# The Gelu table's load behind the last use of ACT in a batch, and the router's rows turned in the banks of the second product

## The reference

```python
edge_index = jnp.stack([src, dst])          # 100000 edges, sorted by dst
x = x + gnn(layernorm(x), edge_index, ...)  # 8 heads
x = x + experts(layernorm(x)[None], ...)[0] # 8 experts, 2 a token
```

```python
out = agg + xn @ W_res + bias
out = layer_norm(out, ln2_g, ln2_b)
ff = gelu_tanh(out @ ffn_w1 + ffn_b1) @ ffn_w2 + ffn_b2   # 256 -> 1024 -> 256
return out + ff
```

## Time and profile before

| | |
|---|---|
| median of 3 executions | 3304.02 us (3302.67 to 3306.39) |
| profiled execution, its own time | 3309.24 us |
| its span | 3307.6 us |
| mean granted clock of TensorE over the span | 0.75 |
| busy: PE, DVE, ACT, POOL | 2076.5, 1683.3, 1450.4, 1175.7 us |
| edges and before | 2204 us |
| layer stage | 413 us |
| experts | 691 us |

### The profile page before, as it was taken

One profiled execution on the slowest core, in us unless ns is written; L12 is line 12 of the kernel. 1 busy time (PEld: TensorE's weight loads), 2 busy tenths in 40 slices (PEclk: granted clock), 3 DMA queues, 4 the chain that ended last, 5 costly groups with the idle time before them and its releaser, 6 DMA issues.

```text
span 3307.6 us, 51219 instructions
## 1 busy us (share of the span) xinstructions
PE 2076.5 (63%) x16490; PEld 1777.0 (54%) x16490; DVE 1683.3 (51%) x5236; ACT 1450.4 (44%) x3212; POOL 1175.7 (36%) x1155
## 2 busy tenths in 40 slices
PE   5334554445544455444554445469899499999999
PEld 4223333334333343333433333358878499999999
DVE  6234554445544455444554445587766445555554
ACT  3313333333333333333333333346665466666665
POOL 2444334433344333443344433301323312222223
PEclk8656666666666666666666666679999799999999
DMA  7633333333333333333333333322222444463533
GB/s 187 174 99 91 96 95 105 112 88 96 95 108 99 98 96 95 109 99 98 94 96 109 99 98 88 95 94 65 91 73 67 136 108 97 77 171 51 146 50 40
DMA packets 268719, 329.50 MB, mean 100 GB/s; under 512 B 118550, under 2 KB 207984, under 8 KB 263716
## 3 DMA queue, kind: packets, MB, share of 16 engines
q0 software_dynamic: 63840, 151.61, 19.3%
q1 hardware_dynamic: 204036, 173.54, 17.5%
q10 hardware_dynamic: 576, 1.09, 0.1%
HBM read 431.90 MB, written 95.53 MB: 159 GB/s over the span
## 4 chain that ended last, share of the span: by engine, by line
PE 41%; another core or an unknown queue 30%; DVE 10%; issue 8%; ACT 7%; DMA 1%; SPq 1%; DVEq 1%; POOL 1%; ACTq 0%; POOLq 0%
PE bank L928 14%; PE bank L1104 7%; PE bank L1105 7%; PE bank L1106 7%; PE bank L917 2%; ACT edge_mem L827 1%; DVE edge_mem L994 1%; ACT layer_hid L1199 1%; DVE seg_max L1031 1%; PE bank L514 1%; ACT layer_mem L1198 1%; DVE win_mem L1020 1%; ACT layer_mem L1207 1%; DVE piece_lo L1100 1%
## 5 line engine op out<-in xcount | busy, mean ns | idle before, releaser
L737 POOL DMA_INDIRECT edge_mem<-node_table,src_col x880 | 836.5, 951 | 1188.9 <-PE bank L928 923.0
L928 PE MATMUL bank<-edge_mem 128*128 128x264 f32 x1760 | 554.5, 488 | 4.6 <-DVE edge_mem L994 3.3
L1104 PE MATMUL bank<-expert_rounded 128*128 128x256 f32 x1792 | 509.0, 284 | 34.9 <-DVE expert_rounded L1100 30.2
L1105 PE MATMUL bank<-expert_rounded 128*128 128x256 f32 x1792 | 508.7, 284 | 0.0
L1106 PE MATMUL bank<-expert_rounded 128*128 128x256 f32 x1792 | 508.5, 284 | 0.0
L1041 DVE TENSOR_TENSOR exponent<-edge_mem,bank 128x128 f32<-128x128 f32 x55 | 15.8, 288 | 928.7 <-remote 926.6
L928 PEld LDWEIGHTS bank<-edge_mem 128*128 128x128 f32 x1760 | 429.6, 249 | 108.2 <-issue 5.0
L917 PE MATMUL bank<-cand,edge_mem 128*128 128x9 bf16 x2640 | 81.2, 169 | 644.0 <-DVE cand L1054 618.0
L843 ACT CAST cand<-bank 128x128 bf16<-128x128 f32 x55 | 14.8, 268 | 1019.2 <-remote 1005.2
L917 PEld LDWEIGHTS bank<-cand,edge_mem 128*128 128x128 bf16 x2640 | 75.4, 104 | 682.6 <-DVE cand L1054 655.6
L1104 PEld LDWEIGHTS bank<-expert_rounded 128*128 128x128 f32 x1792 | 345.7, 193 | 35.1 <-issue 35.1
(11 more groups left out here) (229 smaller groups left out, 3968.0 us busy)
## 6 DMA issues: line engine op xcount, KB each, us to landing
expert_rounded<-split_w SPq DMA_DIRECT2D x224, 1024.0 KB
split_w<-piece_hi SPq DMA_DIRECT2D x72, 256.0 KB
split_w<-piece_lo SPq DMA_DIRECT2D x72, 256.0 KB
piece_full<-in_L_ffn_W SPq DMA_DIRECT2D x64, 256.0 KB
expert_mem<-expert_rows SPq DMA_DIRECT2D x224, 64.0 KB, 2.8
edge_mem<-node_table,src_col POOLq DMA_INDIRECT x880
node_table<-win_mem SPq DMA_DIRECT2D x12, 544.0 KB
xn_in<-turned SPq DMA_DIRECT2D x49, 128.0 KB
```

Of the source, the lines that this page charges most:

```text
L737: pool.indirect_dma_start(gath[g % NGB][:, t, :], None, node_table, bass.IndirectOffsetOnAxis(ap=src_col[:, k, t % 2:t % 2 + 1], axis=0)). ...
L928: ins = pe.matmul(bank[5 + at % 3][:, 0:AGG], onehot[g % 2][:, 2 * k + j, :], gath[g % NGB][:, 2 * k + j, 0:AGG], start=(j == 0), stop=(j ...
L1104: pe.matmul(out_ap, s_hi, m_lo, start=start, stop=False)
L1105: pe.matmul(out_ap, s_lo, m_hi, start=False, stop=False)
```

## The change

ACT gets one more instruction per batch, a Gelu of one column into a tile that nothing reads, behind norm_rows; in an iteration where the next index is a batch. turn_z puts its result into banks 4 and 5, the banks of the second product, for all batches but the last two, which stay in banks 0 and 1. The waits follow: turn_out no longer waits for zT_ready; the first two output tiles wait for the zT copy of their bank; turn_z waits until the output tiles of its own batch have been read (x1_ready), which stood in banks 4 and 5, in place of outT_ready, which it keeps for the last two batches.

```diff
--- before.py
+++ after.py
@@ -253,6 +253,7 @@
         tok = sb2("tok", [P, 4, 4])
         ids = sb2("ids", [P, NT], I32)
         valid = sb2("valid", [P, 1])
+        gelu_probe = sb2("gelu_probe", [P, 1])
         tri = sb2("tri", [P, P])
         tri16, ones16 = sb2("tri16", [P, P], BF16), sb2("ones16", [P, P], BF16)
         middle.close()
@@ -1081,6 +1082,11 @@
         def z_at(b):
             return (2, 5, 6) if b < NB - 1 else (3, 7, 7)
 
+
+
+        def z_bank(b, k):
+            return bank[(4 if b < NB - 2 else 0) + k]
+
         def is_batch(b):
             return 0 <= b < NB
 
@@ -1187,6 +1193,9 @@
                 if is_batch(b - 1):
                     norm_rows(b - 1)
 
+                if is_batch(b + 1):
+                    act.activation(gelu_probe[:, :], ones[:, 0:1], ACT.Gelu_apprx_tanh)
+
         def gelus(b, m):
             n = batch_tiles(b)
             if m == 0 and b >= 1:
@@ -1214,7 +1223,7 @@
                 act.wait_ge(logits_made, b)
             for k in range(KC):
                 act.wait_ge(z_turned, KC * b + k + 1)
-                act.copy(zT[:, k, 0:n * P], bank[k][:, 0:n * P]).then_inc(zT_ready, 1)
+                act.copy(zT[:, k, 0:n * P], z_bank(b, k)[:, 0:n * P]).then_inc(zT_ready, 1)
 
         def scale_outT(b):
             n, i = batch_tiles(b), b % 2
@@ -1325,6 +1334,8 @@
                 pe.wait_ge(x1_ready, w - 1)
             elif b >= 1:
                 pe.wait_ge(x1_ready, tiles_before(b - 1) + 1 + max(q for q in range(batch_tiles(b - 1)) if q % 2 == j))
+            if j < 2 and b >= 1 and b - 1 < NB - 2:
+                pe.wait_ge(zT_ready, KC * (b - 1) + j + 1)
             for m in range(MC):
                 if j == 0:
                     pe.wait_ge(hid_low, MC * b + m + 1)
@@ -1337,20 +1348,21 @@
             for k in range(KC):
                 if b >= 1:
                     pe.wait_ge(outT_ready, KC * (b - 1) + k + 1)
-                if b >= 2:
-                    pe.wait_ge(zT_ready, KC * (b - 2) + k + 1)
                 for j in range(batch_tiles(b)):
                     ins = pe.transpose(bank[k][:, j * P:(j + 1) * P], rows[b % 4][:, j, k * P:(k + 1) * P], ident[:, :])
                 ins.then_inc(out_turned, 1)
 
         def turn_z(b):
             pe.wait_ge(z_ready, b + 1)
+            if b < NB - 2:
+                pe.wait_ge(x1_ready, tiles_before(b + 1))
             for k in range(KC):
-                pe.wait_ge(outT_ready, KC * min(b + 1, NB - 1) + k + 1)
+                if b >= NB - 2:
+                    pe.wait_ge(outT_ready, KC * NB)
                 if b >= 1:
                     pe.wait_ge(zT_ready, KC * (b - 1) + k + 1)
                 for j in range(batch_tiles(b)):
-                    ins = pe.transpose(bank[k][:, j * P:(j + 1) * P], zrow[:, j, k * P:(k + 1) * P], ident[:, :])
+                    ins = pe.transpose(z_bank(b, k)[:, j * P:(j + 1) * P], zrow[:, j, k * P:(k + 1) * P], ident[:, :])
                 ins.then_inc(z_turned, 1)
 
         def logits(b):
```

## The result

| | before | after |
|---|---|---|
| median | 3304.72 us (3300.71 to 3314.55, 20 runs) | 3297.43 us (3289.93 to 3309.72, 20 runs) |
| profiled execution, its own time | 3309.24 us | 3290.94 us |
| its span | 3307.6 us | 3289.3 us |
| batches 2 to 10, in the profiled execution | 290.92 us | 277.49 us |

The ratio is 0.9978, with a 95% interval of 0.9969 to 0.9986: 7.3 us less. The predicted median was 3296.0. So I read positions within a batch from one profile, and times from medians.

What follows compares the result with a forecast made beforehand. A batch was bounded by T to the last scatter (27.9 us), plus 1.1, plus TensorE's rest of the fourth tile. Gains of 3.5 + 4.6 = 8.1 us took the median from 3304.02 to 3296 us, range 3289 to 3302.

Steps and rivals of the forecast that it cites:

- Its first term: Layer stage, batches 2 to 10: moving the Gelu table load earlier gains 9 x 0.39 = 3.5 us.
- its second: Long batches: the clock falls less often, taking half of their 9.13 us excess, 4.6 us.
- Where the load stands, and its cover: ACT: load moves with the probe behind norm_rows, 1.28 us plus about 0.2, covered by 6.75 us idle; 13 loads.
- norm_z 0.39 us earlier: norm_z on ACT starts at 2437.62 instead of 2438.01; statistics, second power, scatters and release all come 0.39 us earlier.
- The banks are worth nothing in a short batch: Output tiles start 0.9 us earlier, but the third waits for VectorE's first add, so short batches gain nothing.
- Half of the long batches' excess goes: Four long batches carry 9.13 us above the short mean; between 0 and 9.1 goes, half taken: 4.6 us.
- rival 1: Clock alternates as before, only the load's share passes: 3300.5 us; chance 0.20.
- No idle before turn_out: TensorE: turn_out starts at the hidden products' end, 1.00 us earlier; 0.2 to 0.4 us idle before the router's products.
- Rival 5: Stall at the scatters: every batch becomes long, 297.8 us for batches 2 to 10, 3311 total; chance 0.06 including unforeseen.
- Rival 4: The table load's full length is on the path in 11 batches, 14.1 us, clock unchanged: 3290 us; chance 0.03.
- rival 3: Each of nine batches gains batch 1's 0.89 us (norm_z at T + 5.46), plus half the long excess: 3291.4; chance 0.09.

Runs made afterwards that it cites:

- z_first: Kernel after with z_scale straight behind z_statistics on VectorE, ahead of the low halves of blocks 0 and 1; chip C: 3303.66 us, ratio to before 0.9965.
- after_again: Kernel after, unchanged, timed and profiled again on chip A: 3296.05 us, ratio to before 0.9983.
- after_third: Kernel after, unchanged, on chip C: 3308.10 us, ratio to before 0.9977.

## Why the prediction was right, and where it wasn't

The median (3296.0 against 3297.43), the sign and the range held, but that the sum came within 1.4 us is luck. Its first term, 3.5 us, came out at 2.1; its second, 4.6 us for a clock that falls less often, isn't borne out by the profiles; and a third, the banks' worth at full clock, was missing and fills the gap.

- **Where the load stands, and its cover**: right, 1.28 + 0.20 us behind norm_rows, 4.88 us of idle left. The count was wrong: 12 loads on the probe's line, not 13; the iteration of batch 0 has no Exp before its probe, so nothing is loaded there.
- **norm_z 0.39 us earlier**: this step failed in size, 0.22 us. "Done before POOL is" was true of the low halves, but I took POOL's power at its old 1.67 us. Moved up, the first low half starts ahead of the power and lengthens it to 2.04 us; z_first gave the 0.37 us back. The rest of the chain (statistics, second power, scatters, release) carried 0.23 us to T + 27.65, so this term was 9 x 0.23 = 2.1 us in place of 3.5.
- **The banks are worth nothing in a short batch**: wrong, and the more instructive miss. My argument, that the third tile waits for VectorE's add at T + 21.6 anyway, holds for that tile. At full clock the fourth tile begins 8.15 us behind the first scatter in both kernels. But the batch ends behind a stall, and at full clock the stall comes after about 80 matmuls from the first scatter. TensorE is 0.45 us further when the scatters begin and waits longer for the third tile after that, so it has fewer matmuls behind it when the fourth tile begins, and the slow steps start later: 9.3 us behind the first scatter in batch 7, 8.8 in batch 6 before. In batches 2 to 8 nine to twelve matmuls of the fourth tile are done at the release (twelve in batch 7, with the slow ones), six in batch 6 before, and as many fewer are left: 1.5 us from the release to the next T (2450.54 to 2452.06) against 2.3 in batch 6 before (2429.40 to 2431.66). The runs show the positions and the counts; that the count of matmuls is what limits TensorE is my reading, and the stall after 66 or 67 matmuls in the batches at a lower clock speaks against it.
- **Half of the long batches' excess goes**: not borne out. The first profile of the kernel after has two long batches, as forecast (0.95 and 0.90), but after_again and after_third have six each with a clock of 0.95 or less, and the one profile of before has five. Nor is the fourth tile begun ahead of the stall in the batches of after_again and after_third where the clock fell in front of the output tiles. The gain can be told without this term: by an estimate from the batches at full clock (31.33 us before, 30.43 after on average), 9 x 0.9 = 8 us, of which 2.1 are the scatters' and the rest the banks', against 7.3 measured. The median speaks against rival 1's 3300.5 us (the interval reaches up to 3300.1), but its mechanism, that the clock falls as often as before, isn't excluded.
- **No idle before turn_out**: right. 0.53 us before the router's products, not 0.2 to 0.4, since the copy of zT came 0.2 us later than I worked out. No output tile waited for zT_ready.
- **Rival 5**, every batch long, didn't come: after_third has the most of it, six batches of nine and 287.55 us in place of the rival's 297.8. Rival 4's full load price is excluded by norm_z. Of rival 3's earlier norm_z, T + 5.46, z_first reaches T + 5.77.

The largest thing was in the prediction and not priced: "a batch's length is T to the last scatter, plus 1.1, plus what is left". Followed one step further, to what stands ahead of the scatters on POOL, it gives the swap that is worth 21 to 30 us over the kernel after on the two chips with the stall, three to four times the change, and nothing on the third.

## What to carry to other kernels

Once a wait is named that ends every iteration, look first at the order on the engine that releases it, before shortening anything that leads there: here two independent pieces of POOL's program stood in the wrong order. When work moves up, check what it will now lie beside, and which of the two starts first. And where the clock falls irregularly, take positions from a profile and times from medians only.

## What the runs showed of the hardware that wasn't expected

- On two of three chips of the experiments, TensorE slows to one instruction in 0.7 us while POOL issues indirect transfers, 5 us into a row of 16 in the edges and about 9 us into a row of eight in the layer stage (not when the eight lie beside the hidden products), and engines that wait for a finished product of TensorE get its signal late: 1.0 to 1.3 us after the last of eight, 2.8 to 3.6 us after the last of 16. On the third neither happens, and the whole kernel takes 2366 us in place of 3303. What differs between the chips isn't known; one session was seen on each.
- POOL's power on 128 x 8 elements takes 1.67 us, and 2.04 where a two-input VectorE instruction started 0.18 us before it.
